# Two attention layers on one core: the softmax sums of the last three halves, and where the second weights are waited for

## The reference

```python
xn  = group_norm(x)                                  # 32 groups, scale and shift
qkv = einsum('bchw,oc->bohw', xn, w_qkv) + b_qkv     # 768 rows: 8 heads of q, k, v with 32 rows each
m   = softmax(einsum('bhcs,bhct->bhst', q * scale, k * scale), axis=-1)
a   = einsum('bhst,bhct->bhcs', m, v)
x   = x + einsum('bchw,oc->bohw', a, w_proj) + b_proj
```

## Time and profile before

| | us |
|---|---|
| median of 3 runs | 2064.45 |
| lowest, highest | 2061.98, 2065.25 |
| profiled execution | 2056.22 |
| its span, first to last instruction | 2054.4 |

### The profile page before, as it was taken

How to read it: one execution, slowest core, us unless ns; L and a number is a source line. 1 busy time by engine, 2 the same in 40 slices (tenths; PEclk the granted TensorE clock), 3 DMA queues, 4 the chain that set the end, 5 groups by cost and what they waited for, 6 DMA issues and landing times.

```text
span 2054.4 us, 30311 instructions
## 1 busy us (share of the span) xinstructions
PE 2019.4 (98%) x10080; PEld 1126.6 (55%) x10080; DVE 1685.3 (82%) x2896; ACT 1246.6 (61%) x2321; POOL 1838.2 (89%) x626
## 2 busy tenths in 40 slices
PE   6999999999999999999999999999999999999998
PEld 3465555655556555565555556555565555655543
DVE  5888888888888888888888888888888888888882
ACT  1556666666666666666566566666666666665664
POOL 2699999999999999999989999999999999999985
PEclk9999999999999999999999999999999999999999
DMA  4354455554456445366454555444564453654431
GB/s 129 73 111 101 96 116 124 118 111 90 109 109 144 103 88 121 84 141 144 103 109 85 122 124 119 106 93 111 108 144 103 88 121 82 143 124 83 106 60 42
DMA packets 217306, 220.31 MB, mean 107 GB/s; under 512 B 167488, under 2 KB 167616, under 8 KB 209344
## 3 DMA queue, kind: packets, MB, share of 16 engines
q1 hardware_dynamic: 207792, 152.84, 32.9%
q0 software_dynamic: 8784, 63.97, 16.1%
q10 hardware_dynamic: 576, 1.57, 0.4%
HBM read 36.32 MB, written 16.78 MB: 26 GB/s over the span
## 4 chain that ended last, share of the span: by engine, by line
PE 87%; DVE 6%; POOL 4%; DMA 1%; issue 1%; ACT 0%; SPq 0%; DVEq 0%; POOLq 0%; ACTq 0%
PE ps_t L398 23%; PE ps_m L425 21%; PE ps_v L449 20%; PE ps_d L480 10%; PE ps_d L495 5%; PE ps_d L488 5%; DVE raw_max L737 3%; POOL acc L906 3%; PE ps_m L471 3%; DMA acc<-pt 1%; DVE ps_m L790 1%; DVE att L795 1%; DVE turned L784 1%; DVE res L806 0%; PE ps_m L480 0%
## 5 line engine op out<-in xcount | busy, mean ns | idle before, releaser
L655 ACT ACTIVATE pt<-ps_t 128x512 f32<-128x512 f32 x2048 | 1119.7, 598 | 752.2 <-PE ps_t L398 712.6
L737 DVE TENSOR_REDUCE raw_max<-ps_m 128x1 f32<-128x512 f32 x2048 | 1331.3, 686 | 270.3 <-PE ps_m L425 268.9
L906 POOL TENSOR_TENSOR acc<-acc,pt 128x2048 f32<-128x2048 f32 x315 | 1442.6, 4580 | 45.1 <-ACT pt L655 1.8
L425 PE MATMUL ps_m<-ks,qs 96*128 96x512 f32 x2048 | 982.2, 480 | 8.3 <-DVE raw_max L737 6.0
L398 PE MATMUL ps_t<-qs,ks 97*128 97x512 f32 x2048 | 841.9, 412 | 1.3 <-ACT pt L655 1.1
L398 PEld LDWEIGHTS ps_t<-qs,ks 97*128 97x128 f32 x2048 | 389.5, 190 | 365.1 <-issue 218.9
L449 PE MATMUL ps_v<-pt,v 128*32 128x512 f32 x4096 | 491.2, 597 | 0.0
L425 PEld LDWEIGHTS ps_m<-ks,qs 96*128 96x128 f32 x2048 | 388.8, 190 | 179.6 <-DVE raw_max L737 99.7
L906 POOL TENSOR_TENSOR acc<-pt 128x2048 f32<-128x2048 f32 x64 | 298.3, 4660 | 70.8 <-ACT pt L655 69.7
L480 PE MATMUL ps_d<-xn,wq 128*128 128x512 f32 x500 | 256.9, 596 | 5.8 <-ACT xn L687 5.8
L449 PEld LDWEIGHTS ps_v<-pt,v 128*32 128x32 f32 x4096 | 113.9, 109 | 257.8 <-issue 184.5
(11 more groups left out here) (50 smaller groups left out, 528.8 us busy)
## 6 DMA issues: line engine op xcount, KB each, us to landing
acc<-pt POOLq DMA_DIRECT2D x61, 1024.0 KB, 9.1
qs<-stage_qh SPq DMA_DIRECT2D x256, 128.0 KB, 2.4
ks<-stage_kh SPq DMA_DIRECT2D x248, 128.0 KB, 2.4
qs<-stage_ql SPq DMA_DIRECT2D x128, 128.0 KB, 2.5
qs<-neg_max SPq DMA_DIRECT2D x1024, 0.5 KB, 2.1
ks<-stage_kl SPq DMA_DIRECT2D x124, 128.0 KB, 2.4
xn<-x_dram SPq DMA_DIRECT2D x16, 512.0 KB, 4.5
res<-x_dram SPq DMA_DIRECT2D x16, 512.0 KB, 4.5
```

The lines of the kernel that those rows point to most:

```text
L425: pe.matmul(ps_m[place % RING][:, :], qs[b][0:KROWS, h, c:c + P], ks[b][0:KROWS, h, kf * HALF:(kf + 1) * HALF], start=True, stop=True).the ...
L655: act.activation(tile_of(half, t)[:, h, :], ps_t[(UNITS * s.n + u) % RING][:, :], ACT.Exp, scale=SCALE).then_inc(exp_done, 1)
L737: dve.tensor_reduce(raw_max[:, e % 2, t, kf:kf + 1], ps_m[MAX_PLACE["max", UNITS * n + w] % RING][:, :], AX.X, ALU.max)\
L906: pool.tensor_tensor(acc[hf][:, :, :], a[:, :, :], tile_of(half, t)[:, :, :], ALU.add).then_inc(pool_added, 1)
```

## The change

- `POOLED_END` is (6, 4) and END is 62, so half 61 is treated as all before it: six POOL adds and an accumulating DMA, and eight PE passes over `acc`. These stand at unit 27 of slot 31 (`LAST_ADDED_SUMS_AT`), where before 24 passes stood at unit 11.
- Half 62: DVE adds tile 7 onto tile 6, head by head (`add_two`, four instructions of 128x512), after unit 36. PE's sum at unit 43 takes `acc` and the added tile: 16 passes for 24.
- Half 63: DVE adds tiles 4 and 5 into tile 2's buffer, after the second output piece (unit 58). PE's sum at unit 59 takes `acc` only (8 passes for 24), and after the slot the added tile (8 passes) ahead of tiles 6 and 7.
- SP no longer waits for the second layer's weights. PE waits for `wq` in slot 14 at unit 38, DVE for `bv` before the first values of image 8, and PE for `wp` before its first use, in slot 18.

```diff
-POOLED_END = (6, 6, 4)
+POOLED_END = (6, 4)
+LAST_ADDED_SUMS_AT = 27
@@ def summed_at(half):
-    return half // NH + hf, (SUMS_AT if half < END else SUMS_AT_END) + (1 - hf) * UNITS // NH
+    at = SUMS_AT if half < END - 1 else LAST_ADDED_SUMS_AT if half < END else SUMS_AT_END
+    return half // NH + hf, at + (1 - hf) * UNITS // NH
@@
+        two_added = sem("two_tiles_added")
+        def added_pair(half):
+            return NT - 2 if half == HALVES - 2 else 2
@@ sync: body
                         load_weights(1)
-                        sp.wait_ge(weights, 64)
...
                         sp.dma_start(wp[:, :, :], w_proj[1]).then_inc(wproj_loaded, 16)
-                        sp.wait_ge(wproj_loaded, 32)
@@ tensor: sums
                         pe.wait_ge(last_tile_added, 16 * (half + 1))
+                    elif t == added_pair(half):
+                        pe.wait_ge(two_added, HG * (half - END + 1))
@@ tensor: dense
                             pe.wait_ge(norm_done, NH * s.n - 1 + r // CT)
+                            if r == 0 and s.j == B + 1:
+                                pe.wait_ge(wproj_loaded, 32)
...
                             pe.wait_ge(xn_done, CT * NH * (s.j + 2))
+                            if s.n == 2 * B - 2:
+                                pe.wait_ge(weights, 64)
@@ tensor: slot
-                                sums(half, (*range(pooled_in(half), NT), POOLED_TILES))
+                                sums(half, (POOLED_TILES, added_pair(half)))
                     if not has_next and u == LAST_SUMS_AT:
-                        sums(HALVES - 1, (*range(POOLED_END[-1], NT - 2), POOLED_TILES), last=False)
+                        sums(HALVES - 1, (POOLED_TILES,), last=False)
@@ tensor: after the slots
+            sums(HALVES - 1, (added_pair(HALVES - 1),), first=False, last=False)
             for t in range(NT - PV_TILES, NT):
@@ vector: v_out
+                if r == 0 and j == B:
+                    dve.wait_ge(weights, 64)
@@ vector
+            def add_two(half, a, b):
+                dve.wait_ge(exp_done, HG * (NT * half + b + 1))
+                out = added_pair(half)
+                dve.wait_ge(pv_done, NT * half + (b if out == a else out) + 1)
+                if out != a:
+                    dve.wait_ge(pool_added, added(half, pooled_in(half) - 1))
+                for h in range(HG):
+                    dve.tensor_tensor(tile_of(half, out)[:, h, :], tile_of(half, a)[:, h, :], tile_of(half, b)[:, h, :],
+                                      ALU.add).then_inc(two_added, 1)
@@ vector: slot
                         project_out(s.j, step - LAST_OUT)
+                        if step == LAST_OUT + CT - 1:
+                            add_two(HALVES - 1, NT - 4, NT - 3)
+                    if not has_next and u == PV_AT + LATER + UNITS // NH:
+                        add_two(HALVES - 2, NT - 2, NT - 1)
```

## The result

| | median us | lowest to highest | runs |
|---|---|---|---|
| before | 2062.65 | 2055.99 to 2065.78 | 17 |
| after | 2068.54 | 2063.21 to 2071.48 | 17 |

The ratio is 1.0029, with a 95% interval of 1.002 to 1.0038: the change costs about 6 us (4 to 8 by the interval). The forecast was 5 us less than before. What happened is rival (1): VectorE adds wait out POOL adds.

A forecast was written before the change was run, and what follows sets the result against it. PE, busy 98% of the span with 87% of the chain, was taken as the bound. Sums -3.79 (lower clock) and slot 17 -1.46 gave -5.25 us, 2059.2 by the median; own range 2057.5 to 2061, whole range 2057 to 2070.5.

The forecast's parts named there:

- rival (1): Half 62, unit 43: each VectorE add waits out a POOL add; +4.5 to +6 us, 2069.5; chance 0.25.
- the DVE adds of half 62: After unit 36: four adds of 0.69, 2.76 us in all, hidden within 5.74 us before PE asks at unit 43.
- Sums of half 61: Slot 31: 24 passes at unit 11 go (-2.83), eight come at unit 27 (+0.90); net -1.93 us by unit 43.
- rival (3): Slot 31, unit 20: half 61's accumulating DMA lands late, losing 3.95 us; total -2.65, 2061.8; chance 0.12 with its neighbour.
- Sums of half 62: Unit 43: PE waits 0.42 us for POOL, then 16 passes for 24; running total -3.81, or -2.88 at lower clock.
- The 0.65 at unit 59: Unit 59, half 63: PE waits 0.65 us for POOL's last add at full clock, or not at the lower clock.
- Sums of half 63: Unit 59: eight passes for 24, eight more after the slot (+0.90), DVE adds hidden; running total -4.07, or -3.79.
- Late waits: Without SP's waits: slot 17's DMA lands before PE asks, -1.46 us (bound 0); slot 14 costs nothing.
- the bound: Slot 14: a DMA landing of 12.2 us would cost PE 0.5; about 10, costing nothing, was taken.

The follow-up runs named there:

- e3: Changed kernel with the second operand of half 62's four DVE adds taken from an idle PSUM bank, leaving tile 7 out; ratio 0.9981 to before.
- e5: Kernel before with only half 61's change: six POOL adds, accumulating DMA, eight passes at unit 27; ratio 0.9991 to before.
- e2: Changed kernel with half 62's four 128x512 DVE adds made one add of 128x2048; ratio 0.998 to before.
- e6: Kernel before with only the DVE adds of half 63 and PE's split sums for it; ratio 0.9999 to before.
- e4: Kernel before with only the late waits for the second layer's weights; ratio 0.9993 to before.
- e1: Changed kernel without DVE adds for half 62, PE summing tiles 6 and 7 itself (24 passes at unit 43); ratio 0.9981 to before.
- e10: e1 with SP's wait for the second weights in slot 14 put back; ratio 0.9969 to before.
- e7: e1 plus two 128x512 DVE adds at unit 36 on SBUF buffers nobody uses or waits for; one run, 2061.03 us.
- e8: Changed kernel with one more wait: POOL starts half 63's first add only after DVE's four adds of half 62; ratio 0.9986 to before.
- e9: Changed kernel with each POOL add of halves 62 and 63 split into two of 128x1024; ratio 0.9999 to before.

## Why the prediction was wrong

**The step that failed** is the one on the DVE adds of half 62: "four of 128x512 ... 4 x 0.69 = 2.76 us ... hidden". The work itself was right; e3 and the adds of half 63 show 2.5 us. What was missing is the hold: 13.98 us, against 5.74 of room. The step's price came from a row of adds that read PSUM and SBUF. It said nothing of two SBUF operands, as the prediction itself states, and the sum goes on as if it did: this instruction was the only one of its kind in the kernel, near the path, beside an engine that is 89% busy. 0.25 for rival (1) was too low. That 2068.54 lies inside the stated range, 2057 to 2070.5, says nothing for the sum: the range reached so far up only to take in this rival.

**Rival (1) was right in its mechanism and near in its size.** It had the adds end 16.5 us after they ask (2014.32 to 2030.8), with three whole POOL adds between them; the run shows 14.0, with the rest of one and two whole ones. The fourth add was free, which the rival did not see: PE's stand leaves POOL without a tile to add. It had +4.5 to +6, and the ratio gives +6. The clock cost more than I had it: it was at 0.50 already for the weighted values ahead of the gap (3.31 us for 1.85), came back (1.00 from 2023 to 2025), and was at 0.50 again through the gap and for the 16 passes behind it.

**Sums of half 61**: -1.93 predicted by unit 43, -2.3 in e5 there and -2.0 over its tail. The second add behind the DMA came 5.64 us after its issue (5.72 predicted), and the landing was quick, 7.1 us in after and 7.8 in e5, so rival (3) did not occur.

**Sums of half 62**: with adds that are not held POOL is late at unit 43, as predicted: PE stood 0.80 us for it in e3, where 0.42 was forecast. The 0.65 at unit 59, forecast for full clock, did not show in e3, where the clock had fallen and PE came later; the prediction has that case. The 0.93 in e2 is another thing, since the hold had lengthened a POOL add there.

**Sums of half 63**: -1.81 + 0.90 = -0.9 without a wait for POOL, -0.9 in e6; the adds in one piece of 2.49 us and hidden, as said.

**Late waits**: in slot 17 the stand went, as predicted: in the eight profiles without SP's two waits the DMA lands after 9.5 to 10.5 us and PE does not stand. But -1.46 was one draw. With the wait of before PE stood 1.46 us in before, 0.41 in e5 and 2.18 in e6. In slot 14 the bound came true and not the value I took: 12.2 us to landing and 0.59 us of standing in after (0.48 in e4), where I had taken 0. The four profiles with SP's wait there land after 7.8 to 8.0, the eight without it after 11.7 to 12.2. From the first accumulating DMA to the tail, the eight need 1887.3 to 1890.0 us, and before, e5 and e6 1889.0 to 1892.1: about 2 us less on average, with a spread of 3 within each group.

Together, the parts other than the adds of half 62 were to give 5.25 us less 0.9 for the eight passes of half 62 that e1 keeps, 4.35; e1 gives 0.0019 x 2061.4 = 3.9, between 1.0 and 6.8 by its interval. That sum was sound as far as this can tell.

**What stays open.** Why the start of the kernel runs at a lower clock in some executions and not in others, up to 8 us apart, wasn't tried. Nor is the clock near unit 43 explained: it fell there in every profile but that of e1. And why e10, whose stage copies in slot 17 start as early as e4's, still had a landing of 11.5 us there is open too.

## What to carry to other kernels

Before VectorE is given an elementwise operation on two SBUF tensors, see what POOL does at that time. Here each such add waited out the POOL add that ran, so four small ones beside long POOL adds can cost four long adds, less what finds a gap. If it must be there, make it one instruction, take one operand from PSUM, or let POOL wait once; each of these won back 0.4 to 0.5% here (e3 leaves a tile out, so what it costs to have the operand in PSUM is not in its time). And a price for an operation whose operands lie elsewhere than in any row is no price: it deserves a bound as wide as the longest instruction next to it, and a chance to match.

## What the runs showed of the hardware

- A VectorE add of 128x512 with both operands in SBUF takes 0.68 to 0.69 us while POOL is idle (2.49 for four in a row), up to 5.03 while POOL adds 128x2048 (4.58 alone), and up to 2.86 while POOL adds 128x1024 (2.38 alone). With one operand in PSUM four take 2.48 beside running POOL adds (e3).
- The hold works on POOL as well: its 4.6 us add took 6.62 beside a 2.15 us VectorE add (e2), 4.90 and 4.75 beside the short ones.
- The rule weighed under rival (1), in the Trainium skill, SBUF — State Buffer, section Who interferes with whom, agrees with these traces in three points: two SBUF inputs (13.98 us against 2.48 with one of them in PSUM), for the whole instruction (5.00), and whichever comes second waits (DVE in after, POOL in e2).
- The engines take turns. In after, e7, e8 and e9, whenever POOL had an add to start, it went next after each single VectorE add; VectorE's adds followed one another only where POOL had nothing to start.
